# Moving the sign ahead of the tanh, and |x| from ScalarE to VectorE, in the likelihood layer of a two-layer convolution kernel

## The reference, cut to what matters

```python
lower = _logits_cumulative(xr - 0.5, ms, bs, fs)
upper = _logits_cumulative(xr + 0.5, ms, bs, fs)
sign = jax.lax.stop_gradient(-jnp.sign(lower + upper))
likelihood = jnp.abs(jax.nn.sigmoid(sign * upper) - jax.nn.sigmoid(sign * lower))
likelihood = jnp.maximum(likelihood, 1e-06)
```

## Time and profile before

| | |
|---|---|
| time, median of 3 runs | 5028.21 us (5019.32 to 5030.57) |
| the profiled execution's own time | 5030.57 us, span 5028.8 us |
| PE busy | 4486.9 us (89%), 38408 products |
| DVE busy | 4209.8 us (84%) |
| ACT busy | 3649.6 us (73%) |
| POOL busy | 693.8 us (14%) |
| mean granted TensorE clock | 0.968 |

### The profile page before, as it was taken

One profiled execution on the slowest core, in us unless ns is written; L12 is line 12 of the kernel. 1 busy time (PEld: TensorE's weight loads), 2 busy tenths in 40 slices (PEclk: granted clock), 3 DMA queues, 4 the chain that ended last, 5 costly groups with the idle time before them and its releaser, 6 DMA issues.

```text
span 5028.8 us, 106046 instructions
## 1 busy us (share of the span) xinstructions
PE 4486.9 (89%) x38408; PEld 2990.4 (59%) x38408; DVE 4209.8 (84%) x5474; ACT 3649.6 (73%) x4008; POOL 693.8 (14%) x751
## 2 busy tenths in 40 slices
PE   4999879998899988999889997899978999799976
PEld 2788427873388733887247872588625886167831
DVE  4898789977999778997789978899688996889966
ACT  1667786768776687776876768766787767866788
POOL 5000300003000030101301012000220002101012
PEclk8999999998999999999899999999999999999988
DMA  2100440114310153001420115200242103410133
GB/s 50 39 20 20 98 101 19 33 32 103 88 30 22 35 114 76 28 28 37 112 75 23 31 43 117 62 26 28 55 116 50 33 20 72 107 46 29 33 80 97
DMA packets 154988, 280.18 MB, mean 56 GB/s; under 512 B 37441, under 2 KB 37825, under 8 KB 152706
## 3 DMA queue, kind: packets, MB, share of 16 engines
q1 hardware_dynamic: 154434, 272.94, 21.7%
HBM read 205.49 MB, written 50.33 MB: 51 GB/s over the span
## 4 chain that ended last, share of the span: by engine, by line
PE 55%; DVE 18%; issue 13%; ACT 9%; DMA 2%; SPq 2%; POOL 1%; DVEq 0%; ACTq 0%; POOLq 0%
PE ps L1293 10%; PE ps L1295 10%; PE ps L1297 10%; PE ps L1084 7%; PE ps L1245 6%; DVE mxp L990 5%; ACT th L654 4%; DVE th L929 3%; DVE arena L985 3%; ACT arena L647 3%; PE ps L1156 3%; PE ps L1170 3%; DVE mxp L975 2%; PE ps L1139 2%; DMA arena<-x2d 2%
## 5 line engine op out<-in xcount | busy, mean ns | idle before, releaser
L1293 PE MATMUL ps<-v_sb,arena 128*128 128x193 f16 x8192 | 2021.5, 247 | 11.4 <-DVE arena L985 11.4
L1295 PE MATMUL ps<-v_sb,arena 128*128 128x192 f16 x8192 | 2030.2, 248 | 0.0
L1297 PE MATMUL ps<-v_sb,arena 128*128 128x193 f16 x8192 | 2014.0, 246 | 0.0
L611 ACT ACTIVATE arena<-ps 128x1024 f16<-128x1024 f32 x1024 | 1049.8, 1025 | 932.9 <-PE ps L1084 932.7
L985 DVE TENSOR_TENSOR arena<-arena 128x1024 f16<-128x1024 f32 x1024 | 1294.2, 1264 | 244.0 <-ACT arena L614 243.7
L990 DVE TENSOR_REDUCE mxp<-ps 128x1 f32<-128x512 f32 x1792 | 1177.2, 686 | 50.3 <-PE ps L1245 40.3
L929 DVE SCALAR_TENSOR_TENSOR th<-th,gates,ps 128x1024 f32<-128x1024 f32 x768 | 950.8, 1275 | 226.5 <-ACT th L654 222.5
L614 ACT ACTIVATE arena<-ps 128x1024 f32<-128x1024 f32 x1024 | 1046.8, 1022 | 0.0
L1295 PEld LDWEIGHTS ps<-v_sb,arena 128*128 128x128 f16 x8192 | 796.1, 97 | 262.0
L654 ACT ACTIVATE th<-ps,biases 128x1024 f32<-128x1024 f32 x768 | 825.4, 1113 | 165.4 <-PE ps L1156 119.6
L1293 PEld LDWEIGHTS ps<-v_sb,arena 128*128 128x128 f16 x8192 | 793.4, 97 | 143.6 <-issue 19.3
(11 more groups left out here) (118 smaller groups left out, 3219.8 us busy)
## 6 DMA issues: line engine op xcount, KB each, us to landing
x<-x2d SPq DMA_DIRECT2D x1152, 64.0 KB, 2.4
arena<-x2d SPq DMA_DIRECT2D x768, 64.0 KB, 2.6
xp<-x_dram SPq DMA_DIRECT2D x18, 1536.0 KB, 13.3
shared<-x_dram SPq DMA_DIRECT2D x64, 384.0 KB, 3.8
x2d<-shared SPq DMA_DIRECT2D x64, 384.0 KB, 3.0
res<-x2d SPq DMA_DIRECT2D x96, 256.0 KB
out_dram<-res SPq DMA_DIRECT2D x96, 256.0 KB
kst<-shared SPq DMA_DIRECT2D x32, 256.0 KB, 5.1
```

The costliest lines, as they stand in the source:

```text
L611: act.activation(e_hi[:, q % 4, :].rearrange("p (k n) -> p k n", k=2), sc, ACT.Exp)
L1293: pe.matmul(acc, eh, v_sb[:, m, 0:C + 1], start=(m == 0 and t % 2 == 0), stop=False, skip_group_check=True)
L1295: pe.matmul(acc[:, 0:C], eh, v_sb[:, m, VW:VW + C], start=False, stop=False, skip_group_check=True)
L1297: ins = pe.matmul(acc, el, v_sb[:, m, 0:C + 1], start=False, stop=(m == MT - 1), skip_group_check=True)
```

## The change

Before: sum, tanh of both, Sign of the sum, subtraction, times sign, Abs with 0.5, result. After: sum, Sign, both halves times sign, tanh of both with scale -0.5, subtraction, times 0.5, |x| as max(-x, x), result. ScalarE loses the Abs (one pass of 128x512 for each of the 96 units of all images). GpSimd goes from three passes to five. VectorE gets one pass, ahead of `result`, which waits on its semaphore. In `phase_a` Sign stands in the slot in which tanh stood, tanh and the difference a slot later, and `result` a slot earlier than before (slot 4u + 8 and not 4u + 9), so no longer in the slot of the next unit's logits. In `phase_b` Sign stands behind pair 4 and tanh behind pair 7; `result` stays at the end of pair 15.

```diff
--- before.py
+++ after.py
@@ -272,6 +272,7 @@
         sign_ready = sem("sign_ready")
         signed_ready = sem("signed_ready")
         half_ready = sem("half_ready")
+        twice_ready = sem("twice_ready")
         dif_ready = sem("dif_ready")
         size_ready = sem("size_ready")
         res_in = [sem(f"res_in{s}") for s in range(XR)]
@@ -515,17 +516,21 @@
                 pool.tensor_tensor(lu_sign[:, :], lu[:, u % LUR, 0, :], lu[:, u % LUR, 1, :], ALU.add
                                    ).then_inc(sum_ready, 1)
 
+            def signs(l, u):
+                pool.wait_ge(sign_ready, l * UNITS + u + 1)
+                pool.tensor_tensor(lu[:, u % LUR, 0, :], lu[:, u % LUR, 0, :], lu_sign[:, :], ALU.mult)
+                pool.tensor_tensor(lu[:, u % LUR, 1, :], lu[:, u % LUR, 1, :], lu_sign[:, :], ALU.mult
+                                   ).then_inc(signed_ready, 1)
+
             def difference(l, u):
-
                 pool.wait_ge(half_ready, l * UNITS + u + 1)
                 pool.tensor_tensor(lu[:, u % LUR, 0, :], lu[:, u % LUR, 1, :], lu[:, u % LUR, 0, :], ALU.subtract
+                                   ).then_inc(twice_ready, 1)
+                twice = pool.compute_val(l * UNITS + u + 1)
+                settle(pool)
+                pool.wait_ge(twice_ready, twice)
+                pool.tensor_scalar(lu[:, u % LUR, 0, :], lu[:, u % LUR, 0, :], 0.5, None, ALU.mult
                                    ).then_inc(dif_ready, 1)
-                now = pool.compute_val(l * UNITS + u + 1)
-                settle(pool)
-                pool.wait_ge(sign_ready, now)
-                pool.wait_ge(dif_ready, now)
-                pool.tensor_tensor(lu[:, u % LUR, 0, :], lu[:, u % LUR, 0, :], lu_sign[:, :], ALU.mult
-                                   ).then_inc(signed_ready, 1)
 
             def phase_a(l, proj):
                 pj = counter(l)
@@ -563,11 +568,14 @@
                         if (s - 5) % 4 == 0:
                             sums(l, u)
                         if (s - 5) % 4 == 1:
+                            signs(l, u)
+                        if (s - 5) % 4 == 2:
                             difference(l, u)
 
             def phase_b(l):
                 for u in range(UNITS - LATER, UNITS):
                     sums(l, u)
+                    signs(l, u)
                     difference(l, u)
 
             phase_a(None, True)
@@ -614,15 +622,14 @@
                 act.activation(e_32[:, q % 2, :].rearrange("p (k n) -> p k n", k=2), sc,
                                ACT.Exp).then_inc(full_ready, 1)
 
+            def sign(l, u):
+                act.wait_ge(sum_ready, l * UNITS + u + 1)
+                act.activation(lu_sign[:, :], lu_sign[:, :], ACT.Sign).then_inc(sign_ready, 1)
+
             def halves(l, u):
 
-                act.wait_ge(sum_ready, l * UNITS + u + 1)
-                act.activation(lu[:, u % LUR, :, :], lu[:, u % LUR, :, :], ACT.Tanh, scale=0.5).then_inc(half_ready, 1)
-                act.activation(lu_sign[:, :], lu_sign[:, :], ACT.Sign).then_inc(sign_ready, 1)
-
-            def size(l, u):
                 act.wait_ge(signed_ready, l * UNITS + u + 1)
-                act.activation(lu[:, u % LUR, 0, :], lu[:, u % LUR, 0, :], ACT.Abs, scale=0.5).then_inc(size_ready, 1)
+                act.activation(lu[:, u % LUR, :, :], lu[:, u % LUR, :, :], ACT.Tanh, scale=-0.5).then_inc(half_ready, 1)
 
             def phase_a(l, proj):
                 pj = counter(l)
@@ -692,9 +699,9 @@
                         u = (s - 5) // 4
                         if 0 <= u < now:
                             if (s - 5) % 4 == 1:
+                                sign(l, u)
+                            if (s - 5) % 4 == 2:
                                 halves(l, u)
-                            if (s - 5) % 4 == 3:
-                                size(l, u)
                     if proj and s + V_LEAD < VB:
                         negative(QK + s + V_LEAD)
                 if proj:
@@ -712,9 +719,9 @@
                             exps(pairs, j * PAIRS + p + 2)
                         if l is not None and j < LATER:
                             if p == 4:
+                                sign(l, UNITS - LATER + j)
+                            if p == 7:
                                 halves(l, UNITS - LATER + j)
-                            if p == 10:
-                                size(l, UNITS - LATER + j)
                         if j + 1 == BLOCKS and p == 5:
                             deviation1(b + 1)
 
@@ -892,6 +899,8 @@
 
             def result(l, u):
                 half = lu[:, u % LUR, 0, :]
+                dve.wait_ge(dif_ready, l * UNITS + u + 1)
+                dve.scalar_tensor_tensor(half, half, -1.0, half, ALU.mult, ALU.max).then_inc(size_ready, 1)
                 dve.wait_ge(size_ready, l * UNITS + u + 1)
                 dve.wait_ge(res_in[u % XR], l * (UNITS // XR) * 16 + (u // XR + 1) * 16)
                 dve.scalar_tensor_tensor(res[:, u % XR, :], half, 1e-6, res[:, u % XR, :], ALU.max, ALU.add
@@ -956,16 +965,16 @@
                         for n in range(4, QK + V_LEAD):
                             query(n)
                 now = UNITS - LATER if proj else UNITS
-                for s in range(SLOTS + (1 if proj else 6)):
+                for s in range(SLOTS + (1 if proj else 5)):
                     if l is not None:
                         if s < SLOTS:
                             gate("h1", s, th1[:, s % HR1, :, :], F1O, t1_ready, h1_ready)
                         if 1 <= s <= SLOTS:
                             gate("h2", s - 1, th2[:, (s - 1) % HR2, :, :], F2O, t2_ready, h2_ready)
-                        if s % 4 == 1 and 5 <= s < SLOTS + 5:
+                        if s >= 5 and s % 4 == 1:
                             logits(l, (s - 5) // 4, not proj)
-                        if s >= 9 and s % 4 == 1 and (s - 9) // 4 < now:
-                            result(l, (s - 9) // 4)
+                        if s >= 8 and s % 4 == 0 and s // 4 - 2 < now:
+                            result(l, s // 4 - 2)
                     if proj and s + V_LEAD < VB:
                         value(QK + s + V_LEAD)
                     if proj:
```

## The result

The changed kernel takes 5096.91 us (median of 4 runs, 5088.8 to 5107.15) against 5029.39 of the kernel before: ratio 1.0139, 95% interval 1.0119 to 1.016. It is slower by 67.5 us; 39 were forecast. The profiled execution took 5108.31 (span 5106.5), longer than any of the four, and the comparison of the two traces has 77.7 us to account for.

What follows compares the result with a forecast made beforehand. The prediction took TensorE and VectorE as level in attention blocks, VectorE and ScalarE as taking turns in phase_a. Attention +29.5, phase_a +12.6 and last image -3.4 gave +38.7, so 5067 us, range 5043 to 5098.

Steps and rivals of the forecast that it cites:

- The parts named for the range: Total time: a halving of 1.27 adds 13, phase_a -13 to +12, block 0 and the pass's bounds -8 to +5.
- I put the whole 0.71 on the path.: End of attention blocks: VectorE's new |x| pass delays the reciprocal by 0.71 us, bounds 0.6 to 0.75.
- The rival of a hidden pass: Attention block's end: VectorE's idle 0.84 after the reciprocal hides the new pass, total 5037; chance 0.12.
- the undisturbed cast: GpSimd's 128x512 cast, 0.61 us at its fastest, taken as nearest to the halving, which had no row at this size.
- The tie: Block 0: GpSimd's first product ends just as VectorE asks; which goes first decides between 0 and 1.1, taken as 0.5.
- The rival of products that always keep VectorE out: Attention blocks: GpSimd's two products run together, VectorE waits 1.27 more in each of 35 blocks, total 5124; chance 0.12.
- The wait of 1.7 in slot 7: Phase_a, first units: ScalarE stands about 1.7 us ahead of the tanh, behind GpSimd's values and two products.
- +1.1: Phase_a, units 0 and 1 of an image: waits behind GpSimd's queue, less Abs and result savings, cost +1.1 us.
- the 12.6: Phase_a, seven images: +1.8 us an image, between 0 and +3.5, makes +12.6.
- ScalarE bound: 11 units x -0.52 = -5.7.: Last image: ScalarE sets the pace, so dropping Abs gains 0.52 us in each of 11 units, -5.7.
- the forecast 2.3: Last image's tail, last sum to last result: Sign, two products and the halving in one serial chain add about +2.3 us.

Runs made afterwards that it cites:

- the third experiment: The changed kernel with the result and its |x| back in slot 4u + 9 of phase_a, behind the next unit's logits: 5138.62 us, ratio 1.0217.

## Why the prediction was wrong

The direction held, and so did the mechanism in the attention blocks; the size did not: 5067 forecast, 5096.91 measured, and the ratio on the median of 5028.21 gives 5098.1, just above the upper end of the range. (The parts named for the range add up to 5046 to 5097, and not to the 5043 to 5098 given.) Of the 39 us between forecast and the two traces, 14 lie in blocks 1 to 4, 4 in block 0, 7 in the last image, 8 in phase_a and 5 between the stages. The last two are within what one execution differs from another: for phase_a see below, and the stretches between the stages, with the start, grew by 1.5 to 11 in the traces of the other eleven runs.

- *|x| in an attention block: "I put the whole 0.71 on the path."* Right. 0.73 alone, 0.73 of 1.02 in the change, and hidden when moved to pair 12. The rival of a hidden pass is out for this place.
- *"The halving has one SBUF input ... I take 0.64, nearest the undisturbed cast, and keep 1.27 for the range."* This is the step that failed. It takes 1.49, more than either. I took the number of inputs for what sets a GpSimd pass, and the row of another operation as nearest. With 1.49 the following sum collides again (0.5 in each of 28 blocks, 14 us: the whole miss in blocks 1 to 4), VectorE stands 1.8 in slot 8, and the tail grows by 0.85. Leaving the halving out altogether gave 27 us.
- *Block 0.* The tie was put at 0.5 of 0 to 1.1. It fell the costly way, GpSimd's second product first, in all seven images. Timeline, block 0:

```profile
761.12 1.27 POOL L522 TENSOR_TENSOR lu<-lu,lu_sign 128x512 f32<-128x512 f32 x1
...
761.16 2.31 DVE L994 TENSOR_TENSOR arena<-arena 128x1024 f16<-128x1024 f32 x1
```

  The product began 0.04 ahead, and VectorE's pass took 2.31. In blocks 1 to 4 VectorE had asked first and got in between. So in these runs neither engine has precedence: who asks first has the port for its pass. The Trainium skill (SBUF — State Buffer, Who interferes with whom) says that issue order decides who blocks, and both cases agree with it. The rival of products that always keep VectorE out happened only here.
- *Phase_a.* The wait of 1.7 in slot 7 was right to the digit (with a negative part of 0.47 and not the 0.4 put in, so the digit is luck). What follows was under-sized: +2.3 to +4.0 for the first unit and -0.6 for the second, +2.9 for the two on average against +1.1. In VectorE's full stretch the sixth distance from logits to logits grew by 0.7 (16.7 against 16.0), as forecast, but the seventh fell from 16.0 to 16.8 to 15.4, since its slot holds no result any more. The fifth has what I did not see in the total: it grew by 1.9 on average, 13 of the 20.7 us. It took 16.6 and 17.1 in two images (15.6 in three of the kernel before), and 19.9 to 22.2 in the other five, in which TensorE waited for a transfer of q, as here in the second image, timeline:

```profile
1267.86 1.01 PE L1238 MATMUL ps<-kst,qst 128*128 128x512 f16 x2 [4.22 <-DMA qst<-shared]
```

  The kernel before had four such waits of over 2.5 us. The run with the result behind pair 12 has the same phase_a and only one of them, and its phase_a grew by 7.0 in place of 20.7. So one execution cannot tell whether the 12.6 was too little as a sum.
- *Last image: "ScalarE bound: 11 units x -0.52 = -5.7."* Wrong as well: +0.9. Units took 15.36 before (the 15.55 of the earlier trace rows is the longest of nine) and 15.41 after. In the first of these units ScalarE was busy 14.74 of 15.36 us (from 4848.36 on) and is now busy 14.22 of 15.41 (from 4922.12 on). The reason is in this timeline of VectorE, TensorE and ScalarE in the last image:

```profile
5011.61 0.69 DVE L906 SCALAR_TENSOR_TENSOR res<-lu,res 128x512 f32<-128x512 f32 x1
...
5012.22 2.46 DVE L938 SCALAR_TENSOR_TENSOR th<-th,gates,ps 128x1024 f32<-128x1024 f32 x2
...
5013.64 1.09 PE L1165 MATMUL ps<-arena,w1s 64*64 64x512 f32 x8 [0.59 <-DVE th L938]
...
5015.13 2.12 ACT L661 ACTIVATE th<-ps,biases 128x1024 f32<-128x1024 f32 x2 [1.39 <-PE ps L1165]
```

  Result and |x| now end slot 4u + 8, ahead of the gate at 5012.22; TensorE's next first-layer product waits 0.59 for the gate, and ScalarE 1.39 for the product. ScalarE has 0.52 less to do and waits longer. The experiment with slot 4u + 11 shows the later units at 14.8 to 14.9 when that is gone. Of the result's move I wrote that it leaves the slot of the next unit's logits. That is true, and worth 42 us as the third experiment shows, but I looked at the slot it left and not at what is queued behind it in the slot it went to.
- *Tail.* Last sum to last result, timeline:

```profile
5091.97 1.26 POOL L516 TENSOR_TENSOR lu_sign<-lu 128x512 f32<-128x512 f32 x1 [4.46 <-DVE lu L896]
...
5101.29 0.69 DVE L906 SCALAR_TENSOR_TENSOR res<-lu,res 128x512 f32<-128x512 f32 x1
```

  9.3 instead of 6.2: +3.1, the forecast 2.3 and the halving's 0.85.

## What to carry to other kernels

A pass that is cheap by its length costs by its place: the same |x| was free behind pair 12, 0.7 us at the block's end, and over 2 us where it pushed the result into GpSimd's sum. Before moving work, find for each engine that shares a port what it will be doing at that moment, and what stands behind the moved pass in its queue. An operation that has no row at its size on an engine should get a range that reaches past the nearest other operation, or be measured by itself first.

## What the runs showed of the hardware that was not expected

- GpSimd multiplied a 128x512 float32 tile by a constant in 1.49 us (median of 96), and added or multiplied two such tiles in 1.27.
- Where a VectorE pass with two SBUF inputs met one of GpSimd's 128x512 passes, one waited for the other's end (VectorE's 1.21 us became 1.51 to 2.31), and a start 0.04 us ahead was enough to go first. VectorE's gates (L938, one input in SBUF and one in PSUM) kept their 1.27 us beside GpSimd's passes.
- A wait of 3.55 us on TensorE was followed by a granted clock of 0.50 (1.2 GHz) over the window from 657 to 661, after 1.00 in the one from 649 to 656; products of one form took 1.99 in place of 1.09. What a late product costs is more than its wait.
